# Expert tiles copied out by halves in two PSUM banks, and another division of the last residuals among the engines

## The reference

```python
x = x + _layernorm(_L0_attn_ref(_layernorm(x), Wq, Wk, Wv, Wo, gamma, beta))   # 16 heads of 64, causal
x = x + _layernorm(_L0_ffn_ref(_layernorm(x), router_w, w1, w2))
...
    logits = xt @ router_w                      # 8 experts
    top_p, top_i = jax.lax.top_k(jax.nn.softmax(logits), 2)
    for e in range(8):
        gate_e = jnp.sum(jnp.where(top_i == e, top_p, 0.0), axis=-1)
        hidden = jax.nn.gelu(xt @ w1[e], approximate=True)      # 128 -> 512
        out = out + gate_e[:, None] * (hidden @ w2[e])          # 512 -> 128
```

## Time and profile before

| | us |
|---|---|
| median of 3 runs | 774.43 (774.01 to 776.05) |
| profiled execution | 777.19 |
| its span in the profile | 775.4 |
| TensorE busy | 720.7 (93%) |
| VectorE busy | 592.5 (76%) |
| ScalarE busy | 525.4 (68%) |
| GpSimd busy | 275.4 (36%) |

### The profile page before, as it was taken

The page is one execution under the profiler, slowest core; times in us unless marked ns, Lnnn a source line. Parts: engine busy times, 40 slices in busy tenths (PEclk is TensorE's granted clock), DMA queues, the critical chain, the costliest instruction groups (busy, mean ns, idle before and its releaser), DMA issues.

```text
span 775.4 us, 18459 instructions
## 1 busy us (share of the span) xinstructions
PE 720.7 (93%) x5954; PEld 606.0 (78%) x5955; DVE 592.5 (76%) x2298; ACT 525.4 (68%) x1751; POOL 275.4 (36%) x404
## 2 busy tenths in 40 slices
PE   4899999999999999999999999999987899999954
PEld 3787778888888888878878788888766889999921
DVE  4668898989898888889898888889895765444316
ACT  4677777777777777777777777777763555555505
POOL 3005354141323323131313323232312677555534
PEclk9999999999999999999999999999997999999978
DMA  8350000000000000000000000000002144322156
GB/s 182 117 118 8 9 8 23 8 22 15 22 12 20 19 11 23 8 23 13 17 16 22 16 15 22 8 23 1 24 13 59 53 108 118 81 73 82 45 167 177
DMA packets 53947, 34.94 MB, mean 45 GB/s; under 512 B 10624, under 2 KB 50560, under 8 KB 53856
## 3 DMA queue, kind: packets, MB, share of 16 engines
q1 hardware_dynamic: 48224, 23.81, 11.9%
q0 software_dynamic: 4544, 9.45, 3.4%
q10 hardware_dynamic: 1088, 0.54, 0.3%
HBM read 20.22 MB, written 13.56 MB: 44 GB/s over the span
## 4 chain that ended last, share of the span: by engine, by line
PE 81%; DVE 8%; ACT 4%; issue 3%; DMA 2%; POOL 1%; DVEq 1%; POOLq 0%; SPq 0%; ACTq 0%
PE PT1O L420 12%; PE SC L406 10%; PE A L599 8%; PE A L426 6%; PE M L385 6%; PE M L387 5%; PE M L386 5%; PE SC L412 5%; PE SC L409 3%; PE PT L433 3%; PE PT L434 3%; PE PT1O L437 3%; PE SC L385 2%; PE SC L387 2%; PE SC L386 2%
## 5 line engine op out<-in xcount | busy, mean ns | idle before, releaser
L1092 ACT ACTIVATE qk<-M 128x512 f32<-128x512 f32 x128 | 76.5, 597 | 139.9 <-PE M L387 139.9
L1098 ACT ACTIVATE prob<-SC,nmax 128x256 f32<-128x256 f32 x256 | 125.6, 491 | 0.0
L420 PE MATMUL PT1O<-pT,v_sb 128*64 128x256 f32 (+1 forms) x1024 | 112.2, 339 | 12.2 <-issue 7.4
L420 PEld LDWEIGHTS PT1O<-pT,v_sb 128*64 128x64 f32 x1024 | 65.7, 136 | 55.0 <-issue 22.4
L708 DVE TENSOR_SCALAR prob<-prob,rden 128x256 f32<-128x256 f32 x256 | 101.7, 397 | 9.1
L1096 ACT ACTIVATE prob<-SC,nmax 128x128 f32<-128x128 f32 x256 | 96.6, 377 | 0.0
L1318 POOL DMA_INDIRECT expert_rows<-v_sb,got x78 | 77.8, 997 | 48.1 <-ACT v_sb L1188 31.0
L406 PE MATMUL SC<-qk 64*128 64x256 f32 x512 | 91.0, 432 | 0.8 <-ACT qk L1092 0.8
L1310 POOL DMA_INDIRECT sent_rows<-rec,slot x64 | 64.0, 1001 | 72.4 <-DVE slot L868 54.4
L702 DVE TENSOR_REDUCE nmax<-SC 128x2 f32<-128x512 f32 x128 | 87.1, 680 | 0.0
L385 PE MATMUL M<-xt_hi,wqk_hi 128*128 128x256 f32 x256 | 83.9, 328 | 1.3 <-DVE xt_lo L697 1.3
(11 more groups left out here) (183 smaller groups left out, 1780.6 us busy)
## 6 DMA issues: line engine op xcount, KB each, us to landing
got<-sent_rows SPq DMA_DIRECT2D x39, 132.0 KB, 2.3
w_in<-expert_rows SPq DMA_DIRECT2D x16, 256.0 KB, 4.1
x_in<-L_attn_x SPq DMA_DIRECT2D x16, 128.0 KB, 2.1
w_in<-L_ffn_w SPq DMA_DIRECT2D x1, 2048.0 KB, 12.1
x_res<-L_attn_x SPq DMA_DIRECT2D x16, 128.0 KB, 2.1
w_sb<-L_ffn_w SPq DMA_DIRECT2D x8, 256.0 KB, 4.5
out<-y_out SPq DMA_DIRECT2D x8, 256.0 KB, 2.4
sent_rows<-pad_rec SPq DMA_DIRECT2D x11, 132.0 KB, 4.3
```

Source lines behind the costliest of these rows:

```text
L420: last = mm(O[k * E:(k + 1) * E, cols], v_sb[:, t, h * E:(h + 1) * E], src[:, k, :], start=(t == 0), stop=(t == 1), skip_group_check=True)
L1098: a.activation(prob[:, par, k, P:3 * P], SC[par][:, k, LATE_Q], ACT.Exp, bias=nmax[:, par, k:k + 1], accum_out=den[:, par, k:k + 1]).then_ ...
```

## The change

**Tiles.** `down` writes the first half to bank A and, from tile 8 on, the second to bank M (`two_banks`); tiles 0 to 7 keep both in A (`one_bank`), since M is still in use by the last batches. `out_mm` and `yo_done` now count halves. From tile 9 on each half of `down` waits only for the copy of the same half of the tile before; ScalarE copies each half when it is there, and GpSimd stores each half when it is copied. The number of products, copies and stores is the same.

**The end.** The first group is added by VectorE from `zz` into a tile in SBUF, `z_first`, and TensorE adds groups 1 to 7. SP's load of group 4 waits for that addition. Moments, `shift` and `zn` have four places (o0 to o3). The residuals of even groups stay with VectorE, those of odd groups go to GpSimd, each with its own semaphore and its own place of `y_out`.

```diff
-        zn = hidT[:, 0].rearrange("p c r -> p (c r)").rearrange("p (s k d) -> p s k d", s=2, k=GT)
+        zn = hidT[:].rearrange("p s c r -> p (s c r)").rearrange("p (s k d) -> p s k d", s=4, k=GT)
...
+        one_bank, two_banks = (A[:, 0:D], A[:, D:2 * D]), (A[:, 0:D], M[:, 0:D])
+        def z_tile(g, t):
+            return z_first[:, t, :] if g == 0 else sum_bank[g % 4][:, t * D:(t + 1) * D]
...
                 if g + 4 < NG:
-                    sp.wait_ge(sem("z_sum"), g + 1)
+                    if g == 0:
+                        sp.wait_ge(sem("z_first"), 1)
+                    else:
+                        sp.wait_ge(sem("z_sum"), g)
                     load_results(g + 4)
...
+            def down(n, s, e, halves):
                 pe.wait_ge(sem("gelu"), 2 * n + 2)
-                if isinstance(n, int) and n == 0:
-                    pe.wait_ge(sem("att_done"), B)
-                else:
-                    pe.wait_ge(sem("yo_done"), n)
                 w2_e = w2f[:, bass.ds(e, F)]
                 for t in range(2):
+                    if isinstance(n, int) and n == 0:
+                        pe.wait_ge(sem("att_done"), B)
+                    elif halves is one_bank or (isinstance(n, int) and n == RING):
+                        pe.wait_ge(sem("yo_done"), 2 * n)
+                    else:
+                        pe.wait_ge(sem("yo_done"), 2 * n - 1 + t)
...
+                    last.then_inc(sem("out_mm"), 1)
...
-            for g in range(NG):
+            for g in range(1, NG):
                 pe.wait_ge(zz_ld[g % 4], 16 * K * (g // 4 + 1))
...
+                    if g == 0:
+                        dve.wait_ge(zz_ld[0], 16 * K)
+                        v.tensor_tensor(z_first[:], zz[:, 0, 0], zz[:, 0, 1], ALU.add).then_inc(sem("z_first"), 1)
+                        dve.drain()
+                    else:
+                        dve.wait_ge(sem("z_sum"), g)
...
-                    if g >= 2:
-                        dve.wait_ge(sem("zn_done"), g - 1)
+                    if g >= 4:
+                        dve.wait_ge(sem("zn_done"), g - 3)
...
-                if g >= 2:
+                if g >= 2 and g % 2 == 0:
                     h = g - 2
...
+            def gated(n, k, it, halves):
                 for t in range(2):
+                    act.wait_ge(sem("out_mm"), 2 * n + 2 if halves is one_bank else 2 * n + 1 + t)
...
             def store(n, k):
-                pool.wait_ge(sem("yo_done"), n + 1)
-                q.sem_inc(sem("store_turn"), 1)
                 for t in range(2):
+                    pool.wait_ge(sem("yo_done"), 2 * n + 1 + t)
+                    q.sem_inc(sem("store_turn"), 1)
...
+                if g >= 2 and g % 2 == 1:
+                    h = g - 2
+                    pool.wait_ge(sem("zn_done"), h + 1)
+                    if h >= 2:
+                        pool.wait_ge(out_st[1], 16 * (h // 2))
+                    q.tensor_tensor(y_out[:, 1], x1[:, h * GT:(h + 1) * GT, :], zn[:, h % 4], ALU.add)\
+                        .then_inc(y_out_done[1], 1)
```

More of the change, by code:

```diff
@@ L109, in sandwich_kernel @@
         hT = sb("hT", [P, S])
-        shift = sb("shift", [P, 2, GT])
+        shift = sb("shift", [P, 4, GT])
+        z_first = sb("z_first", [P, GT, D])
         x1 = sb("x1", [P, NT, D])
@@ L202, in sandwich_kernel @@
         out_st = [sem(f"out_st{k}") for k in range(2)]
+        y_out_done = [sem(f"y_out_done{k}") for k in range(2)]
         v_mm, v_done = sem("v_mm"), sem("v_done")
@@ L588, in up @@
                         last.then_inc(sem("up_mm"), 1)
-            def down(n, s, e):
+            def down(n, s, e, halves):
                 pe.wait_ge(sem("gelu"), 2 * n + 2)
-                if isinstance(n, int) and n == 0:
-                    pe.wait_ge(sem("att_done"), B)
-                else:
-                    pe.wait_ge(sem("yo_done"), n)
                 w2_e = w2f[:, bass.ds(e, F)]
                 for t in range(2):
+                    if isinstance(n, int) and n == 0:
[4 more added lines that the diff above has]
+                        pe.wait_ge(sem("yo_done"), 2 * n - 1 + t)
                     for c in range(NF):
[L599 to L602, removed]
+                        last = mm(halves[t], hidT[:, s, c, t * P:(t + 1) * P],
+                                  w2_e[:, c * D:(c + 1) * D], start=(c == 0 and (t == 0 or halves is two_banks)),
+                                  stop=(c == NF - 1), skip_group_check=True)
+                    last.then_inc(sem("out_mm"), 1)
             def ahead_step(it, k):
@@ L617, in ring @@
                     ahead_step(it, k)
-                    down(it * RING + k, k % 2, e[k])
+                    down(it * RING + k, k % 2, e[k], two_banks)
             offsets = []
@@ L639, in epilogue_tile @@
                 else:
-                    down(n, n % 2, offsets[n])
+                    down(n, n % 2, offsets[n], one_bank)
             over_batches(batch)(pe)
@@ L1171, in batch @@
                         else:
-                            gated(n, n, 0)
+                            gated(n, n, 0, one_bank)
             def gelu(n, s):
@@ L1177, in gelu @@
                     if not (isinstance(n, int) and n < 2):
-                        act.wait_ge(sem("out_mm"), n - 1)
+                        act.wait_ge(sem("out_mm"), 2 * n - 2)
                     a.activation(hidT[:, s, 2 * u:2 * u + 2, :].rearrange("p c r -> p (c r)"), SC[s][:, u, :],
                                  ACT.Gelu_apprx_tanh).then_inc(sem("gelu"), 1)
[L1182 to L1186, removed]
+            def gated(n, k, it, halves):
                 for t in range(2):
-                    last = a.activation(yo[:, k, t, :], out_bank[:, t * D:(t + 1) * D], ACT.Copy,
-                                        scale=got[:, k, t, C_GATE:C_GATE + 1])
-                last.then_inc(sem("yo_done"), 1)
+                    act.wait_ge(sem("out_mm"), 2 * n + 2 if halves is one_bank else 2 * n + 1 + t)
+                    if t == 0 and not (isinstance(it, int) and it == 0):
+                        act.wait_ge(back_st[k], 32 * it)
+                    a.activation(yo[:, k, t, :], halves[t], ACT.Copy, scale=got[:, k, t, C_GATE:C_GATE + 1])\
+                        .then_inc(sem("yo_done"), 1)
             def tile_step(it, k):
@@ L1195, in tile_step @@
                     gelu(n + 1, (k + 1) % 2)
-                gated(n, k, it)
+                gated(n, k, it, two_banks)
             over_batches(batch)(act)
@@ L1380, in _ @@
             stores(LOOP_END, TILES)
[L1382 to L1387, removed]
+            for g in range(NG + 2):
+                if g < NG:
+                    o = f"o{g % 4}"
+                    pool.wait_ge(sem("mv_o"), g + 1)
+                    q.tensor_tensor(ve[o][:], mv[o][:, :, 1], ln_eps[:], ALU.add).then_inc(sem("ve_o"), 1)
+                    pool.wait_ge(sem("ve_o"), g + 1)
+                    q.tensor_tensor(rstd[o][:], ve[o][:], half[:], ALU.pow).then_inc(sem("rstd_o"), 1)
+                if g >= 2 and g % 2 == 1:
+                    h = g - 2
+                    pool.wait_ge(sem("zn_done"), h + 1)
[3 more added lines that the diff above has]
+                        .then_inc(y_out_done[1], 1)
 _INS = ["L0_attn_x", "L0_attn_Wq", "L0_attn_Wk", "L0_attn_Wv", "L0_attn_Wo", "L0_attn_gamma", "L0_attn_beta",
```

37 lines of the change are left out of this document (18 added, 19 removed).

## The result

| | before | changed |
|---|---|---|
| median of 11 runs each, same chip, us | 775.95 (772.11 to 777.48) | 779.34 (775.9 to 782.23) |
| profiled execution, us | 777.19 | 781.55 |
| its span, us | 775.4 | 779.8 |

The measured ratio is 1.0047 [1.0032, 1.0062] (the medians alone differ by 3.4 us): the change makes the kernel slower by 0.5%, 3.6 us. Forecast was no difference, +0.5 us, in a range up to +3.5.

What follows compares the result with a forecast made beforehand. TensorE was taken to bound the expert tiles, a loop of VectorE, GpSimd, ScalarE and stores the end. Terms -1.6 - 0.2 + 0 + 2.3 = +0.5 us on the median 774.43 gave 774.9 us, range 772.2 to 777.9.

Steps and rivals of the forecast that it cites:

- Halves in the middle: Tiles 8 to 38: one more TensorE wait and signal per tile cost nothing; bound above 2.5 us over 31 tiles.
- The rival of TensorE's waits: Tiles: the wait inside `down` costs 0.08 us in each of 31 tiles, giving 777.4 us; chance 0.12.
- Last stores: Last tiles: GpSimd's last store starts at 740.1 instead of 741.68, -1.6 us for all that follows.
- Tiles 0 to 7: One-bank tiles: the store of the first half may go sooner, -0.2 us, bounds 0 and -0.3.
- The first sum: End: TensorE starts with group 1, loaded later, at the low clock; +1.3 us for shift 0 and every later sum.
- GpSimd's addition: End: each 128x512 residual on GpSimd takes 1.26 us, bounds 0.69 and above 1.95.
- the rival of 1.95 us each: End: GpSimd's additions stand behind VectorE's, place 1's cycle is 0.7 longer four times, giving 777.7 us; chance 0.10.
- VectorE behind GpSimd: End: if shifts 3 and 6 wait behind GpSimd's residuals, the end costs nearer +2.9 us; without that, +1.7.
- The odd path: End: residual 1 follows root 3, then place 1 of `y_out` cycles in 3.7 us; at least +1.0 us, up to +2.6.
- Four places for moments: End: VectorE no longer waits for ScalarE before `bn_aggr`; gain counted inside the other times.
- The whole end: From first sums to last store: +2.3 us taken, range +1.0 to +2.9.
- The faster rival: End: residuals 1 and 3 slip in early, pace 1.7 instead of 2.1 us a group, giving 771.1 us; chance 0.14.

Runs made afterwards that it cites:

- e1: Kernel before with only the tiles' halves in two banks, the end left as before; ratio to before 0.9973 [0.9955, 0.9990].
- e5: Changed kernel plus twelve TensorE products that nobody reads, ahead of its sums at the end; ratio to before 1.0026 [1.0009, 1.0043].
- e7: Changed kernel with all eight residuals on VectorE, none on GpSimd, two places of `y_out`; ratio to before 0.9986 [0.9970, 1.0003].
- e3: Kernel before plus one GpSimd 128x4 addition with unused result after the last residual; ratio to before 1.0034 [1.0015, 1.0053].
- e4: Changed kernel with only the last residual, 7, moved back to VectorE; ratio to before 0.9997 [0.9977, 1.0016].
- e9: Kernel before plus halves in two banks, four places for moments and for `y_out`, eleven unread TensorE products before the sums; ratio to before 0.9944 [0.9920, 0.9968].
- e6: Changed kernel with group 0 summed by TensorE again, no `z_first`; ratio to before 1.0031 [1.0014, 1.0047].
- e10: Kernel before plus halves in two banks and four places for moments, without unread TensorE products; ratio to before 0.9987 [0.9969, 1.0006].
- e2: Kernel before with only the changed end, the tiles left as before; ratio to before 1.0082 [1.0053, 1.0111].

## Why the prediction was wrong, point by point

- **Halves in the middle, 0.** Right: 3.45 us from `down` to `down`, no wait, and e1 excludes the 2.5 us of the bound. The rival of TensorE's waits falls.
- **Last stores, -1.6.** Right: -1.57 in the trace, and e1's ratio gives -2.1 us, with an interval (-3.6 to -0.8) that holds it. GpSimd paid its 0.30 from the second store on, not 0.80.
- **Tiles 0 to 7, -0.2.** Not seen: `down` 37 started 0.17 us later, not earlier. It is too small to matter.
- **The first sum, +1.3.** This step failed in its words "and for every later sum". For the first sum it held: 3.8 us at the low clock, statistics of group 1 at 10.5 us after the first load, 10.6 by the forecast. But I took the clock to rise as soon after TensorE's start as before. It took 5.7 us in place of 3.4, the second sum was slow too, and group 2 was 2.2 us late, not 1.3. e5 shows what the low clock costs in this arrangement: 2.6 us of stretch, 1.6 by the ratios.
- **GpSimd's addition, 1.26.** Right to the hundredth, and the rival of 1.95 us each falls.
- **VectorE behind GpSimd.** Both sides were on the table: 0.77 us of a VectorE scaling inside a GpSimd operation, which had one tensor input, and by the rule "+2.9". I chose between. The rows of the change decide: each of shifts 3, 5 and 7, 128x4 with two inputs in SBUF, took 1.2 us and ended with GpSimd's residual; in e7 none did. In the Trainium skill ("SBUF — State Buffer", section "Who interferes with whom") such a VectorE instruction waits for all of GpSimd's. By that rule, the trace agrees; I had named shifts 3 and 6, and it was 3, 5 and 7.
- **The odd path.** The mechanism was right: residual 1 after root 3, residual 5 after roots 6 and 7, residual 7 waiting 2.33 us for the store of group 5. Its pace was not: I let place 1's cycle of 3.7 us go round three times, and residuals 1, 3 and 5 came 4.47 us apart, only the last after 3.60. They were paced by the round of two groups, into which a shift of 1.2 us had come, and not by the place: residuals 3 and 5 started within 0.1 us of the end of the root ahead of them (768.40 + 1.01 for residual 5 at 769.37).
- **Four places for moments.** I gave them no term of their own, and no run shows a gain of theirs.
- **The whole end, +2.3.** This is the step that failed. It came out as +5.8 (31.4 to 37.2). Up to the last landing it is +3.2, 0.9 more than I took. The other 2.6 I did not have at all: the sum ends with "its store landed 2.3 later, 774.6", as though the program were over with the last store. GpSimd's DRAIN was in the trace of before, 6.37 us long and ending at 775.2 in a span of 775.4, so it even set the end there; I had not looked at line 56. Moving the last residual to GpSimd put 5.3 us behind that residual, and 0.3 more to the end, where its store needed 2.3 to land. e3 shows it by itself, e4 by taking it away.
- **The faster rival** (GpSimd's residuals slip in, the pace is TensorE's) didn't occur; 1.94 us a group came only in e9, with other means.

With the DRAIN, +2.6, in the sum, the forecast would have been 777.5, outside my bound for "same" and inside the range. The +2.9 of the other side comes within 0.3 of the measured +3.2, in part by luck: it was worked out with shifts 3 and 6 and without the second slow sum. How the +3.2 divides between the low clock and GpSimd's residuals is not separated: the 2.6 us of e5 and the 1.8 of e7 against e4 together exceed it, so they seem to overlap.

What stays open: what decides when the clock rises. Where TensorE began with group 0 it rose 3.2 to 3.4 us after the start (before, e1, e3; idle for 8.6 to 8.9 us ahead of it) or 4.8 to 5.2 (e6, e10; idle for 8.5). Where it began with group 1 it rose after 5.3 to 6.2 us (the change, e2, e4, e7; idle for 10.8 to 11.3). That would fit a dependence on the idle time or on the start, but e6 and e10 had been idle no longer than e1. No run varied one of these alone, and of each kernel one execution was profiled, so that part of the spread may be chance: over the eleven executions of the changed kernel the mean granted clock went from 0.975 to 0.985 and the span from 780.5 to 774.1 us.

## What to carry to other kernels

Look at the closing rows of each engine before giving it the last operation of a program: here 5.3 us follow GpSimd's last one, so its last operation should end at least that long before the last landing. Put GpSimd's long SBUF operations where VectorE has none with two SBUF inputs on the path; an addition that saves VectorE 0.69 us held it up by 1.1. And where an engine's first piece of work after a pause is on the path, count the pieces that run at the low clock after it, in a trace with that pause.

## What the runs showed of the hardware

- GpSimd's DRAIN at the end of the program ends 5.3 to 5.4 us after its last operation, whatever that was: a power of 128x4 (before, 769.86 to 775.2), an addition of 128x512 (changed, 774.23 to 779.5; e4, 786.03 to 791.4), an addition of 128x4 (e3, 786.65 to 791.95). The span ends 0.1 to 0.3 us after it in all twelve kernels. The DRAINs of TensorE, VectorE and ScalarE here take 0.7 to 2.0 us in all, that of SyncE 0.007.
- A VectorE operation of 0.13 us takes 1.2 us when it starts just after a GpSimd addition of 1.26 us has begun, and the two end together.
- After a pause of 8.5 to 11.3 us TensorE's granted clock is 0.50 (1.2 GHz) and goes to 1.00 (2.4 GHz) 3.2 to 6.2 us after it begins again; with products in the pause it stays at 1.00, and from TensorE's start to VectorE's statistics the first sum takes 1.9 to 2.0 us (e9, 746.62 to 748.54; e5, 749.38 to 751.41) in place of 3.8.
